# Row sums of the first graph layer in 220 visits of two slots, with a one-operation one-hot and a written-out loop

## What is computed

```python
gathered = edge_val[:, None] * x[edge_col]
support = jax.ops.segment_sum(gathered, edge_row, num_segments=N)   # edge_row = src, edge_col = dst
h = jnp.concatenate([x, support], axis=1)
out = h @ W + b
```

## Time and profile before

| | us |
|---|---|
| median of 3 runs | 2531.91 (2526.62 to 2535.03) |
| the profiled execution | 2526.24 |
| its span, first to last instruction | 2524.4 |
| stage 3 of it, SP's first register load to the end of the last addition | 683.7 to 928.6 |
| TensorE / VectorE / ScalarE / GpSimd busy over the span | 79% / 66% / 54% / 60% |

### The profile page before, as it was taken

One profiled execution on the slowest core, in us unless ns is written; L12 is line 12 of the kernel. 1 busy time (PEld: TensorE's weight loads), 2 busy tenths in 40 slices (PEclk: granted clock), 3 DMA queues, 4 the chain that ended last, 5 costly groups with the idle time before them and its releaser, 6 DMA issues. The chain is left out here.

```text
span 2524.4 us, 37785 instructions
## 1 busy us (share of the span) xinstructions
PE 1983.8 (79%) x8650; PEld 1357.8 (54%) x8650; DVE 1668.5 (66%) x3532; ACT 1364.3 (54%) x5328; POOL 1519.3 (60%) x1740
## 2 busy tenths in 40 slices
PE   0665666566399989599999999958489999999975
PEld 0443444444277776356666666634256666666644
DVE  9534333333266667388888888866278888888866
ACT  0355555555300003177777877764157877777773
POOL 3377777777600008877766666619877666666602
PEclk9777777877699999899999999988799999999997
DMA  3387575655498962355555555621255555555532
GB/s 97 81 192 169 169 168 173 165 167 168 117 267 265 270 191 71 101 158 155 149 146 158 147 144 146 134 66 39 72 155 154 148 144 149 146 144 149 139 89 96
DMA packets 272019, 369.89 MB, mean 147 GB/s; under 512 B 40436, under 2 KB 230902, under 8 KB 271831
## 3 DMA queue, kind: packets, MB, share of 16 engines
q1 hardware_dynamic: 207159, 195.75, 28.0%
q0 software_dynamic: 64512, 171.82, 24.9%
q10 hardware_dynamic: 160, 0.20, 0.0%
HBM read 272.59 MB, written 101.50 MB: 148 GB/s over the span
## 5 line engine op out<-in xcount | busy, mean ns | idle before, releaser
L1132 POOL DMA_INDIRECT gath<-gather_table,SRCI x880 | 840.2, 955 | 351.0 <-issue 245.1
L1343 ACT ACTIVATE gath<-gath 128x32 f32<-128x32 f32 x3520 | 766.3, 306 | 0.0
L1178 PE MATMUL p_sums<-gath,OH 128*128 128x272 f32 x1760 | 473.4, 408 | 67.5 <-issue 25.2
L733 POOL DMA_INDIRECT rows_by_src<-gath,node x440 | 438.5, 997 | 137.7 <-issue 116.5
L1146 PE MATMUL p_expd<-gath,ident 128*128 128x512 f32 x880 | 425.3, 606 | 65.5 <-DMA gath<-gather_table,SRCI 65.0
L667 PE MATMUL p_expd<-X,HOTS 128*128 x880 | 302.5, 505 | 219.8 <-DVE HOTS L626 215.8
L1178 PEld LDWEIGHTS p_sums<-gath,OH 128*128 128x128 f32 x1760 | 318.9, 193 | 173.4 <-issue 75.9
L667 PEld LDWEIGHTS p_expd<-X,HOTS 128*128 128x128 f32 x880 | 210.8, 250 | 300.6 <-issue 264.0
L1206 DVE SCALAR_TENSOR_TENSOR work<-p_expd,VEC 128x512 f32<-128x512 f32 x440 | 283.1, 685 | 115.6 <-PE p_expd L1151 109.0
L1151 PEld LDWEIGHTS p_expd<-node,LBC 128*128 128x128 bf16 x2640 | 258.6, 98 | 152.1 <-issue 127.1
L1151 PE MATMUL p_expd<-node,LBC 128*128 x2640 | 324.3, 273 | 0.0
(11 more groups left out here) (285 smaller groups left out, 2251.7 us busy)
## 6 DMA issues: line engine op xcount, KB each, us to landing
gath<-rows_by_src SPq DMA_DIRECT2D x122, 514.0 KB
LBC<-hots_by_node SPq DMA_DIRECT2D x220, 128.0 KB
HOTS<-hots_by_edge SPq DMA_DIRECT2D x220, 128.0 KB, 2.4
LBC<-local_rows SPq DMA_DIRECT2D x110, 128.0 KB
hots_by_node<-gath SPq DMA_DIRECT2D x110, 128.0 KB
hots_by_edge<-gath SPq DMA_DIRECT2D x110, 128.0 KB, 2.9
gath<-gather_table,SRCI POOLq DMA_INDIRECT x880, 3.0
rows_by_src<-gath,node POOLq DMA_INDIRECT x440
```

Source lines behind the costliest of these rows:

```text
L733: pool.indirect_dma_start(sup_d[:, :], bass.IndirectOffsetOnAxis(POSI[:, i:i + 1], 0), U[:, q % 4, g, :], None, bounds_check=EP - 1, oob_i ...
L1132: pool.indirect_dma_start(ROWS[:, i % (RING * G), 0:XW], None, tab_d[:, :], bass.IndirectOffsetOnAxis(SRCI[:, i:i + 1], 0)).then_inc(gathe ...
L1178: ins = pe.matmul(sums[k][:, 0:RW], OH[:, a % 2, g, :], slots(a, g, g + 1)[:, 0, :], start=(g % 2 == 0), stop=(g % 2 == 1))
L1343: ins = act.activation(R[:, h * C:(h + 1) * C], R[:, h * C:(h + 1) * C], ACT.Copy, scale=R[:, D + h:D + h + 1])
```

## The change

Four things change together, all for stage 3.

- **Groups of two slots.** A visit takes two slots, so there are 392/2 + 24 = 220 visits. Each loads 257 KB and has two matmuls. The ring has eight places of two slots instead of four of four, so as many bytes as before.
- **One-hot by one operation.** `iota_row + FIRST == node number` in one scalar_tensor_tensor over 128 x 256, instead of a subtraction, a wait for it, and a comparison over 128 x 512. Four one-hots are held instead of two, and the addition follows three visits behind instead of two. VectorE waits for GpSimd's clearing ahead of everything instead of ahead of its first addition.
- **Loop written out.** SP, VectorE and TensorE have all 220 visits as straight code.
- **Visit tables elsewhere.** 220 entries don't fit in the 128-word tables. `JROW` and `FIRST` now lie in an unused part of `node`; the count takes two operations instead of one, the store to DRAM has 110 partitions by 2 words instead of 128 by 1.

```diff
-VS = EB // G + NJ
+VS = EB // 2 + NJ
...
-        JROW = sb("JROW", [1, P], I32)
+        JROW = node[0:1, 13312:13312 + VS].bitcast(I32)
...
-        FIRST = sb("FIRST", [P, P], FP32)
+        FIRST = node[:, 13312 + VS:13312 + 2 * VS]
...
-                    sp.dma_start(step_d[0, NI:].rearrange("(p a) -> p a", a=1), JI[:, G:G + 1],
+                    sp.dma_start(step_d[0, NI:].rearrange("(g p) -> p g", p=IR), JI[0:IR, G:G + 2],
                                  allow_slow_non_contiguous=True).then_inc(visits_stored, 16)
                     sp.wait_ge(visits_stored, 16)
-                    sp.dma_start(JROW[0:1, :], step_d[:, NI:]).then_inc(visits_back, 16)
-                    sp.dma_start(TI, step_d[:, NI:].broadcast_to([P, P])).then_inc(visits_back, 16)
+                    sp.dma_start(JROW, step_d[:, NI:]).then_inc(visits_back, 16)
+                    sp.dma_start(TI, step_d[:, NI:].broadcast_to([P, VS])).then_inc(visits_back, 16)
...
-                    link(dve.tensor_scalar(JUNK[:, 0:NJ], VB, iota_p[:, 0:1], 0.0,
-                                           ALU.is_le, ALU.add, accum_out=JC[:, G:G + 1]))
-                    dve.tensor_copy(JI[:, G:G + 1], JC[:, G:G + 1]).then_inc(visits_ready, 1)
+                    for g in range(2):
+                        link(dve.tensor_scalar(JUNK[:, 0:NJ], VB, step_no[:, g:g + 1], 0.0,
+                                               ALU.is_le, ALU.add, accum_out=JC[:, G + g:G + g + 1]))
+                    dve.tensor_copy(JI[:, G:G + 2], JC[:, G:G + 2]).then_inc(visits_ready, 1)
...
-            U = gath[:, 0:4 * G * UW].rearrange("p (s g w) -> p s g w", s=4, g=G)
+            DEEP = 8
+            U = gath[:, 0:DEEP * 2 * UW].rearrange("p (s g w) -> p s g w", s=DEEP, g=2)
...
-                    def one(v, s, turn, past):
-                        j = sp.value_load(JROW[0:1, bass.ds(v, 1)], min_val=0, max_val=NJ)
-                        m = group_of(v - j, EB // G - 1)
-                        if past == 4:
-                            sp.wait_ge(sum_ready, v - 3)
+                    for v in range(VS):
+                        s = v % DEEP
+                        j = sp.value_load(JROW[0:1, v:v + 1], min_val=0, max_val=NJ)
+                        m = group_of(v - j, EB // 2 - 1)
+                        if v >= DEEP:
+                            sp.wait_ge(sum_ready, v - DEEP + 1)
                         sp.dma_start(U[:, s], sup_rows[bass.ds(m, 1)].rearrange("a p g w -> (a p) g w")).then_inc(rows_in[s], 16)
-                    visits(sp, one)
...
-                        dve.wait_ge(rows_in[s], 16 * (turn + 1))
-                        if past >= 2:
-                            dve.wait_ge(sum_ready, v - 1)
-                        dve.tensor_tensor(LS[:, s % 2, :], U[:, s, :, D], FIRST[:, bass.ds(v, 1)].broadcast_to([P, G]), ALU.subtract).then_inc(loc_ready, 1)
-                        dve.wait_ge(loc_ready, v + 1)
-                        dve.tensor_tensor(OH[:, s % 2], iota_row[:, :].unsqueeze(1).broadcast_to([P, G, P]),
-                                          LS[:, s % 2, :].unsqueeze(2).broadcast_to([P, G, P]), ALU.is_equal).then_inc(hot_ready, 1)
+                        dve.wait_ge(rows_in[s], 16 * (v // DEEP + 1))
+                        if v >= 4:
+                            dve.wait_ge(sum_ready, v - 3)
+                        dve.scalar_tensor_tensor(HOT[:, v % 4], iota_row[:, :].unsqueeze(1).broadcast_to([P, 2, P]), FIRST[:, v:v + 1],
+                                                 U[:, s, :, D:UW].broadcast_to([P, 2, P]), ALU.add, ALU.is_equal).then_inc(hot_ready, 1)
...
+                    dve.wait_ge(cleared, 1)
+                    for v in range(VS):
+                        hots(v)
+                        if v >= 3:
+                            add(v - 3)
...
-                        for g in range(G):
-                            ins = pe.matmul(sums[s][:, 0:D], OH[:, s % 2, g, :], U[:, s, g, 0:D], start=(g == 0), stop=(g == G - 1))
+                        for g in range(2):
+                            ins = pe.matmul(sums[v % 4][:, 0:D], HOT[:, v % 4, g, :], U[:, v % DEEP, g, 0:D], start=(g == 0), stop=(g == 1))
                         ins.then_inc(sum_ready, 1)
```

More of the change, by code:

```diff
@@ L229, in build @@
             VBJ = small[:, 480:480 + NJ].bitcast(I32)
-            JC = small[:, 512:512 + G + 1]
-            JI = small[:, 520:520 + G + 1].bitcast(I32)
+            JC = small[:, 512:512 + G + 2]
+            JI = small[:, 520:520 + G + 2].bitcast(I32)
             BIX = small[:, 528:528 + G].bitcast(I32)
@@ L457, in _ @@
                     dve.wait_ge(visits_back, 32)
[L458 to L459 removed]
+                    link(dve.tensor_copy(T[:, 0, 0:VS], TI))
+                    dve.tensor_scalar(FIRST, T[:, 0, 0:VS], float(P), None, ALU.mult)
                     dve.wait_ge(trans, 6)
@@ L741, in build @@
         with ctx:
-            U = gath[:, 0:4 * G * UW].rearrange("p (s g w) -> p s g w", s=4, g=G)
-            LS = ctx.enter_context(nc.sbuf_tensor("src_local", [P, 2, G], FP32))
+            DEEP = 8
+            U = gath[:, 0:DEEP * 2 * UW].rearrange("p (s g w) -> p s g w", s=DEEP, g=2)
+            HOT = OH[:, :, :, :].rearrange("p s (b g) n -> p (s b) g n", g=2)
             sums = [ps(f"sums{k}", [P, 512]) for k in range(4)]
-            rows_in = [sem(f"rows_in{k}") for k in range(4)]
@@ L746, in build @@
[L746 to L749, removed]
-            with nc.Block() as block:
-                def visits(eng, one):
-                    for s in range(4):
-                        one(s, s, 0, s)
-                    with eng.Fori(1, turns) as it:
-                        for s in range(4):
-                            one(4 * it + s, s, it, 4)
-                    for v in range(4 * turns, VS):
-                        one(v, v % 4, turns, 4)
+            rows_in = [sem(f"rows_in{k}") for k in range(DEEP)]
@@ L787, in add, with hots @@
-                    def add(v, s, past):
-                        j = dve.value_load(JROW[0:1, bass.ds(v, 1)], min_val=0, max_val=NJ)
+                    def hots(v):
+                        s = v % DEEP
+                        dve.wait_ge(rows_in[s], 16 * (v // DEEP + 1))
[3 more added lines that the diff above has]
+                                                 U[:, s, :, D:UW].broadcast_to([P, 2, P]), ALU.add, ALU.is_equal).then_inc(hot_ready, 1)
@@ L789, in add @@
+                    def add(v):
+                        j = dve.value_load(JROW[0:1, v:v + 1], min_val=0, max_val=NJ)
                         dve.wait_ge(sum_ready, v + 1)
-                        if past:
+                        if v:
                             dve.wait_ge(added, v)
-                        dve.tensor_tensor(SUP[:, bass.ds(j, 1), :], SUP[:, bass.ds(j, 1), :], sums[s][:, 0:D].unsqueeze(1), ALU.add).then_inc(added, 1)
-                    def one(v, s, turn, past):
-                        hots(v, s, turn, past)
-                        if past == 2:
-                            dve.wait_ge(cleared, 1)
-                        if past >= 2:
-                            add(v - 2, (s - 2) % 4, past - 2)
@@ L800, in _ @@
-                    visits(dve, one)
-                    for v in (VS - 2, VS - 1):
-                        add(v, v % 4, 3)
+                        dve.tensor_tensor(SUP[:, bass.ds(j, 1), :], SUP[:, bass.ds(j, 1), :], sums[v % 4][:, 0:D].unsqueeze(1), ALU.add).then_inc(added, 1)
+                    dve.wait_ge(cleared, 1)
[3 more added lines that the diff above has]
+                            add(v - 3)
+                    for v in range(VS - 3, VS):
+                        add(v)
@@ L812, in one @@
                         ins.then_inc(sum_ready, 1)
-                    visits(pe, one)
         XT = gath[:, 8 * D:12 * D].rearrange("p (s w) -> p s w", s=2)
```

9 lines of the change are left out of this document (5 added, 4 removed).

## The result

The changed kernel takes **2558.7 us** (median of 4 runs, 2556.7 to 2560.0) against 2533.5 us (2526.6 to 2536.3) for the kernel before: a ratio of 1.0103, with an interval of 1.0081 to 1.0125. It is slower by one per cent, where 2559.5 was forecast. Repeated later on another chip it was 1.0093 [1.0074, 1.0113].

A forecast was written before the change was run, and what follows sets the result against it. TensorE and DMA engines were both near their limit; afterwards SP's issuing would set the pace. Stage 3 +26.1 and stage 1 +1.5 make +27.6 us, put on 2531.91: 2559.5 us, range 2534 to 2580.

The forecast's parts named there:

- The first rival: Stage 3: SP's issue work stays hidden and transfers set the pace at 0.98 us a visit; total 2513 us, chance 0.09.
- The term of 1.20 us: Stage 3, SP: register work and DMA issue take 1.20 us per load; 217 intervals make 260.4 us.
- Rival 2: Stage 3: SP and VectorE overlap register work better, a visit takes 1.09 us; total 2536 us, chance 0.06.
- Landing and tail: End of stage 3: last landing 3.0 us, then one-hot to addition and the trailing additions, 3.8 us.
- The new wait for the clearing: Start of stage 3: VectorE's first one-hot waits for GpSimd's clearing; at most 1.5 us delay, absorbed by the ring, price 0.
- The sum for stage 3: Stage 3: first issue, SP's intervals, landing and tail put the last addition at 954.7 instead of 928.58 us, +26.1 us.
- Stage 1: Visit tables: store of 220 words +1.1 us by a straight line, extra counting 0.3, wider table 0.1; +1.5 us.
- The forecast for the new one-hot: Stage 3, VectorE: one scalar_tensor_tensor over 128 x 256 takes 0.426 us, replacing 0.16 + 0.69 and a gap.
- Its 1.17: Stage 3, VectorE's visit if the register load begins only once the one-hot has started; 0.95 if begun while it is queued.
- rival 3: Stage 3: VectorE sets the pace with a visit of 1.30 us or so; 22 us more, 2581, chance 0.09.
- Two signs: Stage 3 profile: VectorE waits for landings at most visits, a few hundredths to 0.25 us; TensorE busy for about 0.74.
- Rival 4: Stage 3: TensorE falls to 1.2 GHz, a visit takes 1.77 us; time near 2680 us, chance 0.02.

## Why the prediction was right

**The sign and the mechanism hold.** SP's register work around 220 issues sets the pace of stage 3. Read from the profile after (0.3 us of waiting on SP), it was then shown by experiments in both directions: more work on SP comes out in full, less of it releases the gain, and less work on VectorE does nothing.

**The first rival was right about the gain and wrong about SP.** The tenth fewer slots and the smaller visits are there: with sequencers relieved, stage 3 takes 202 us. The changed kernel gives all of it back in issue time. The prediction set the Trainium skill's rule (DMA: Bandwidth & Descriptors, "Issuing engines are not separate DMA queues"), that the time to initiate a DMA is usually small against the DMA, against the row, and took the row. A usual visit of SP, 1.20 us, stands against 0.87 us for moving 257 KB once nothing else is in the way, and a second sequencer took 56 us off stage 3. Against the 3.1 us from issue to landing 1.20 is the smaller, but landings overlap and issues of one sequencer don't. For DMAs whose address is read from memory each time, the rule does not hold here.

**The term of 1.20 us** was 1.197 in the median: three written-out visits of the old kernel priced 217 new ones. What it lacked are the pauses. Each 18.3 visits an interval is 0.36 us longer, 12 times, and the second of the stage is 0.30 longer, some 4.6 us in all. The prediction had one long issue and, as its upper end, one more in each eight visits (1.26); the measured mean, 1.218, lies between. The low end of 1.15 stood on an issue that gets cheaper with the rows: it took 0.373 us, as before. Rival 2, a visit of 1.09, isn't seen: of 219 intervals only the last is under 1.18. From the first issue to the last are 266.8 us where 263.3 were forecast.

**Landing and tail** were put at 6.8 us; from the last issue at 953.5 to the end of the last addition at 960.57 are 7.1. The last rows of VectorE, beside the earlier trace rows:

```profile
957.32 0.42 DVE L781 TENSOR_TENSOR node<-node,p_sums 128x256 f32 x1
958.15 0.42 DVE L781 TENSOR_TENSOR node<-node,p_sums 128x256 f32 x1 [0.40 <-DVE node L781]
958.98 0.42 DVE L781 TENSOR_TENSOR node<-node,p_sums 128x256 f32 x1 [0.41 <-DVE node L781]
960.15 0.42 DVE L781 TENSOR_TENSOR node<-node,p_sums 128x256 f32 x1 [0.76 <-DVE node L781]
```

Of the three additions that trail, two are 0.83 apart, as said, and the last is 1.17 behind, with a gap of 0.35 after its register work; what held it was not tried. The new wait for the clearing held the first one-hot to 691.3 us and cost nothing, as said: SP waited for 0.3 us in the whole stage. The end lies at 960.6 and not at 954.7, but 2.1 us of that are a stage 2 that was longer by as much in this execution.

**The sum for stage 3** was +26.1; between the first profiles it is +29.9, between the second ones 276.4 - 249.9 = +26.5, and the medians allow 25. Its size is right within what the kernel before varies by.

**Stage 1 was mis-sized.** +1.5 us was forecast and +0.1 measured. Profiles of the old table's code end stage 1 at 98.5 to 100.2 us (4 of them), those of the new one at 98.6 to 100.3 (9), so no cost can be told. The step that failed is the straight line between the stores of 128 and of 440 words:

```profile
88.48 0.30 SPq L300 DMA_DIRECT2D step_tables<-prep_small  x1
...
93.95 0.23 SPq L303 DMA_DIRECT2D node<-step_tables  x1
...
98.29 0.28 DVE L459 CAST work<-node 128x220 f32<-128x220 int32 x1 [2.48 <-DMA node<-step_tables]
```

From the store to the load back are 5.5 us for 220 words, less than the 6.6 for 128; over all profiles it is 5.5 to 6.2 for 220 words and 5.9 to 7.3 for 128. More words did not take longer. In the first two profiles the store is issued 1.6 us later and waits for less; both loads back start near 93.8. What they wait for in common isn't settled: indirect transfers of GpSimd land at the same time, at 94, but nothing was tried on it, nor on the store's partitions (110 instead of 128).

**The time itself** came closer (2558.7 for 2559.5) than the steps deserve. Forecast was a difference of 27.6, and the medians differ by 25.3, on a median of before that came out 1.6 higher than the one then known. The pauses were missing (4.6, of which the one long interval that was kept covers 0.46), stage 1 was 1.4 too high, and the rest is within the 4 us by which stage 3 of before varies.

**VectorE.** The forecast for the new one-hot, 0.426 us from an operation of the same size in stage 4, was too low by 0.06:

```profile
L773 DVE SCALAR_TENSOR_TENSOR OH<-iota_row,node,gath x220: 477/483/486, 691.3 to 956.7; 128x256 f32<-128x256 f32 x110
```

Both take two tensors and a scalar and give 128 x 256 results. What sets this one apart is an operand that repeats one column 128 times and a scalar that is read from a column, where the other has a constant; which of the two costs the 0.057 us was not tried. It cost nothing, as VectorE's visit is 0.935 and SP's 1.2. That 0.935 is near the 0.95 that the prediction had called possible and not believed. Its 1.17 is in the trace too, but the read that causes it waits for the landing and not for the one-hot, so it comes only where VectorE is ahead of its rows. Once it falls behind it has 0.935, and rival 3, which wanted 1.30 at every visit, did not come. The margin under SP was 0.26 us a visit and not 0.03.

**Two signs need a second look.** VectorE was to wait for landings at most visits, for a few hundredths to 0.25 us. The view of waits has 35, but it leaves out idle times under 0.15 us. By the records the one-hot starts within 0.03 us of the landing at half of the visits, and at 93 VectorE had stood idle for it: the sign came, at a little under half of the visits. The idle time ahead of the additions, 55 us, is put down to TensorE and "issue" by the view. TensorE had finished each sum at least 0.5 us and in the median 2.7 us before; an addition starts 0.81 us after the start of its own register read, and it is this path that it waits for.

TensorE was to be busy for 0.74; it shows 0.90. A matmul's record has 0.38 us in this kernel and in the kernel before, but only 0.217 us pass from one start to the next when TensorE is full. When it isn't, the record's length covers part of the idle time. 293 records in 90 us at 0.217 are 0.71, which is near the forecast of 0.74. The DMA share (0.77 for 0.73, 218 GB/s for 219) and the clock (1.00) were as described.

```profile
L798 PE MATMUL p_sums<-gath,OH x880: 377/379/796, 691.9 to 958.0; 128*128 128x256 f32 x176
```

**Rival 4** (TensorE at 1.2 GHz) did not come: the granted clock is 1.00 in the middle of the stage. In the run with the doubled register read, with 206 records in the same 90 us, it is 0.94, a mixture of the two levels, and is not needed to explain that run's time.

## What to carry over

A load whose address is read from memory costs its sequencer a fixed time (here 1.20 us for seven instructions), whether it brings 257 or 514 KB; before making transfers smaller and more numerous, subtract the waits from the span of that sequencer's issues and compare what is left per visit with the new visit. An engine that the profile shows idle can be the next bound by its sequencer alone. And reading four addresses with one instruction costs hardly more than reading one (0.304 us for 0.272), so the finer tiling paid once this had been done, and the range check dropped with it: 2481.7 us for 2533.1.

## What the runs showed of the chip

**Straight code pauses SP.** In the changed kernel SP's issues are 0.36 us late once each 18.3 visits, which at seven instructions a visit are 128 instructions; counted in the records, a gap of 0.34 to 0.36 us stands after every 128th, wherever in the visit that falls. With the second read there are ten instructions a visit, and the pauses come each 12.8 visits: 128 instructions again. They follow the count of instructions, not of transfers. The queues that bring instructions moved 141 and 78 packets after, where before they moved 117 and 71:

```profile
q8 instruction: 78, 1.28, 0.2%
q14 instruction: 141, 1.16, 0.1%
```

1.16 MB in 141 packets are 8.2 KB each, or 64 bytes for each of 128 instructions. In stage 3 of the changed kernel a packet of q14 follows each of the 12 pauses by 0.7 to 1.8 us. And in the run with SP's visits in a loop a gap of this length is there once, in the loop's first turn; later turns have only one of 0.21 us, behind the branch at their end. That the pause is such a fetch is inferred from this; no run was made for it.

**Issue time did not follow size here.** The issue took 0.374 us for 514 KB in four rows per partition and 0.373 us for 257 KB in two. One row per partition was issued in 0.320.

**Cost of reads into registers.** On SP 0.272 us for one word and 0.304 for four; on VectorE 0.302 and 0.343.

**What lets VectorE's sequencer run ahead.** Its register read passed a one-hot that waited for its engine (0.21 us ahead at 801.3), and never one that waited for a landing (0 of 216 visits of the changed kernel).

**DMA rate.** Rows of 1028 bytes moved at 301 GB/s with the DMA engines at 0.99, where the kernel before had 269 GB/s at 0.91. Whether the smaller visits or the ring of eight places brought that was not taken apart.
